# A vision tower on one core: heads of a product-key layer moved between gathering and multiplying, and a scan's sums moved to TensorE

## The reference

```
# 1 tokens: every 4 x 4 patch is averaged; softmax attention of the mean over its 16 pixels, 8 heads
# 2 two-way selective scan, 128 channels, 16 states, over 256 tokens, forward and backward:
for t: h = exp(delta[t] * A) * h + (delta[t] * u[t]) * B[t];  y[t] = sum over 16 states of C[t] * h
# 3 product keys, 8 heads:
scores, idx = top_k(q @ keys of side 0 and of side 1, 16 each of 64)
score = 16 x 16 sums; final_scores, final_indices = top_k(score, 16); softmax
k, v = sum of 16 weights times rows of a table of 4096 rows per head, 64 + 64 wide
out  = causal attention of 256 tokens per head with this k and v, then Wo
```

## Time and profile before

| | |
|---|---|
| median of 3 runs | 13356.86 us (13354.56 to 13362.06) |
| the profiled execution | 13354.71 us, span 13352.6 us |
| TensorE (PE) busy | 11719.0 us, 88% |
| its weight loads (PEld) | 9286.1 us, 70% |
| VectorE (DVE) | 10428.1 us, 78% |
| ScalarE (ACT) | 7363.4 us, 55% |
| GpSimd (POOL) | 10215.8 us, 77%, 9220 instructions |
| mean granted TensorE clock | 0.933 |

### The profile page before, as it was taken

How to read it: one execution, slowest core, us unless ns; L and a number is a source line. 1 busy time by engine, 2 the same in 40 slices (tenths; PEclk the granted TensorE clock), 3 DMA queues, 4 the chain that set the end, 5 groups by cost and what they waited for, 6 DMA issues and landing times.

```text
span 13352.6 us, 262103 instructions
## 1 busy us (share of the span) xinstructions
PE 11719.0 (88%) x71396; PEld 9286.1 (70%) x71396; DVE 10428.1 (78%) x39940; ACT 7363.4 (55%) x17030; POOL 10215.8 (77%) x9220
## 2 busy tenths in 40 slices
PE   3888888988989889989889888898888888898988
PEld 3677677776777767777767677776677677776776
DVE  7878778778778787787777877877878878778772
ACT  2555555555555555555555555555555555555554
POOL 1777777777777777777777777777777777777776
PEclk6999999999999999999999999999999999999999
DMA  2555555555555555555555555555555555555554
GB/s 73 160 145 153 157 145 154 154 144 159 145 151 158 144 154 153 147 156 148 149 159 146 151 159 143 155 154 146 157 143 153 159 145 153 158 142 157 152 140 120
DMA packets 1668219, 1983.98 MB, mean 149 GB/s; under 512 B 532846, under 2 KB 1134062, under 8 KB 1666286
## 3 DMA queue, kind: packets, MB, share of 16 engines
q1 hardware_dynamic: 1371566, 1359.71, 35.8%
q0 software_dynamic: 294912, 604.57, 17.5%
HBM read 1898.00 MB, written 65.01 MB: 147 GB/s over the span
## 4 chain that ended last, share of the span: by engine, by line
PE 38%; DVE 26%; POOL 18%; issue 11%; DMA 4%; ACT 2%; SPq 0%; DVEq 0%; POOLq 0%; ACTq 0%
POOL gath L801 18%; PE bank L991 9%; PE bank L1032 6%; PE bank L873 4%; PE bank L1019 3%; DVE apart L1701 3%; PE bank L1006 3%; DVE row_f L1704 3%; DMA gath<-in_table_dram,rowsT 2%; DVE decay L1576 2%; PE bank L954 2%; DVE onehot L1803 2%; PE bank L977 2%; PE bank L1050 1%; DMA moving<-keyspace 1%
## 5 line engine op out<-in xcount | busy, mean ns | idle before, releaser
L801 POOL DMA_INDIRECT gath<-in_table_dram,rowsT x9216 | 10215.6, 1108 | 3105.9 <-issue 2673.7
L1256 ACT ACTIVATE weight<-bank 128x512 f32<-128x512 f32 x3584 | 2139.3, 597 | 4415.0 <-PE bank L1006 4383.9
L991 PE MATMUL bank<-weight,rowtab 128*128 128x256 f32 x12288 | 3373.8, 399 | 0.0
L1032 PEld LDWEIGHTS bank<-spread,gath 128*128 128x128 f32 x18432 | 2519.7, 201 | 727.8 <-DMA gath<-in_table_dram,rowsT 607.6
L1032 PE MATMUL bank<-spread,gath 128*128 128x96 f32 x18432 | 2524.3, 282 | 519.0 <-DMA gath<-in_table_dram,rowsT 518.8
L991 PEld LDWEIGHTS bank<-weight,rowtab 128*128 128x128 f32 x12288 | 2460.7, 202 | 620.3 <-issue 102.2
L1249 ACT ACTIVATE bank<-bank,seventeen 128x512 f32<-128x512 f32 x3584 | 2370.6, 661 | 13.3 <-PE bank L1006 10.2
L1019 PE MATMUL bank<-moving,pick_b 96*128 96x512 bf16 x3584 | 1457.5, 407 | 304.7 <-ACT bank L1249 226.5
L1006 PE MATMUL bank<-moving,pick_b 96*128 96x512 bf16 x3584 | 1435.0, 400 | 71.1 <-DMA moving<-keyspace 70.6
L1568 DVE TENSOR_TENSOR_SCAN decay<-decay,wide 128x1024 f32<-128x1024 f32 x512 | 1169.3, 2285 | 26.4
L1836 DVE SCALAR_TENSOR_TENSOR acc<-bank,rrow,acc 128x64 f32<-128x64 f32 x1024 | 240.5, 276 | 839.3 <-PE bank L1006 797.2
(11 more groups left out here) (268 smaller groups left out, 18929.9 us busy)
## 6 DMA issues: line engine op xcount, KB each, us to landing
rowtab<-in_tableD_dram SPq DMA_DIRECT2D x2048, 256.0 KB
wide<-states SPq DMA_DIRECT2D x512, 512.0 KB
moving<-keyspace SPq DMA_DIRECT2D x3072, 64.0 KB
gath<-in_table_dram,rowsT POOLq DMA_INDIRECT x9216
pix<-in_x_dram SPq DMA_DIRECT2D x504, 256.0 KB
moving<-keyspace SPq DMA_DIRECT2D x3072, 32.0 KB
keyspace<-split SPq DMA_DIRECT2D x192, 256.0 KB, 2.1
moving<-keyhalf SPq DMA_DIRECT2D x512, 64.0 KB
```

The lines of the kernel that those rows point to most:

```text
L801: pool.indirect_dma_start(out=gath[:, u % RING, j, :], out_offset=None, in_=table, in_offset=bass.IndirectOffsetOnAxis(ap=rowsT[k][:, col: ...
L991: mm(dense_ps[:, 0:TOK], rowtab[:, r, s % 2 * 2 + half, :], weight[s % 2][:, half * TOK:(half + 1) * TOK], start=(s % 16 == 0 and half == ...
L1032: mm(sums_ps[:, col:col + STREAM], gath[:, u % RING, j, :], flat[:, col:col + STREAM], start=True, stop=True)
L1256: ins = af(weight[s % 2][:], zd_ps[s % 2][:], ACT.Exp, scale=-1.0)
```

## The change

`DENSE` goes from 3 to 4: heads 0 to 3 are dense in full (64 slots a period), heads 4 to 7 are gathered (32 parts, 128 fetches). The half head with its own functions, its DRAM buffer `keyhalf`, its semaphores and the items `S.X5`, `S.selh`, `S.l2`, `S.R8`, `S.R9`, `S.wb4`, `k4` and `g4` goes. The number of table tiles streamed stays 32. The gather ring shrinks from 6 parts to 4. In the scan VectorE's half sums (L1577) go, and TensorE sums 32 products (two directions of 16 states), not 16. The four plans are written anew for 64 slots.

```diff
-DENSE = 3
+DENSE = 4
-HU = DU + TILES
+HU = DU
-SLOTS = 16 * DENSE + 8
+SLOTS = 16 * DENSE
-PARTS = (GH * SPAN - SPAN // 2) // PART
-RING = 6
+PARTS = GH * SPAN // PART
+RING = 4
...
                     for r in range(2):
                         hs = decay[r][:, q * 4 * TOK:(q + 1) * 4 * TOK]
-                        after(step(v.tensor_tensor(hs, hs, quarter[q], ALU.mult)))
-                        last = v.tensor_tensor(hs[:, 0:2 * TOK], hs[:, 0:2 * TOK], hs[:, 2 * TOK:4 * TOK], ALU.add)
+                        last = v.tensor_tensor(hs, hs, quarter[q], ALU.mult)
                     last.then_inc(c_done, 1)
...
-                    n = c // 2 * 4 + c % 2
-                    for r in range(2):
-                        mm(scan_ps[:, r * TOK:(r + 1) * TOK], ident[:], decay[r][:, n * TOK:(n + 1) * TOK],
-                           start=(n == 0 and r == 0), stop=False, skip_group_check=True)
+                    for n in (2 * c, 2 * c + 1):
+                        for r in range(2):
+                            mm(scan_ps[:, r * TOK:(r + 1) * TOK], ident[:], decay[r][:, n * TOK:(n + 1) * TOK],
+                               start=(n == 0 and r == 0), stop=False, skip_group_check=True)
...
-                if h < DENSE:
-                    mm(dense_ps[:, 0:TOK], rowtab[:, r, s % 2 * 2 + half, :],
-                       weight[s % 2][:, half * TOK:(half + 1) * TOK],
-                       start=(s % 16 == 0 and half == 0), stop=(s % 16 == 15 and half == 1),
-                       skip_group_check=True)
-                else:
-                    for q in (2 * half, 2 * half + 1):
-                        mm(dense_ps[:, 0:P], rowtab[:, r, q, :], weight[s % 2][:, q * P:(q + 1) * P],
-                           start=(s % 16 == 0 and q == 0), stop=(s == SLOTS - 1 and q == 3),
-                           skip_group_check=True)
+                mm(dense_ps[:, 0:TOK], rowtab[:, r, s % 2 * 2 + half, :],
+                   weight[s % 2][:, half * TOK:(half + 1) * TOK],
+                   start=(s % 16 == 0 and half == 0), stop=(s % 16 == 15 and half == 1),
+                   skip_group_check=True)
```

Of the plans, the lines that the prediction speaks of (TensorE's, VectorE's and SP's):

```diff
 PE_ORDER
-21 z20+0 a0.6+0 o21+0 d19+0 g1.5+0 a1.0+0
-28 z27+0 a1.6+0 o28+0 d26+0 a2.0+0
-39 z38+0 o39+0 d37+0 g3.1+0 S.E1+1
-55 z54+0 o55+0 d53+0 S.E2+1 F.y+2
+0 z63-1 o0+0 d62-1
+16 z15+0 o16+0 d14+0
+25 z24+0 o25+0 d23+0 g1.4+0 a0.6+0
+26 z25+0 o26+0 d24+0 a1.0+0
+33 z32+0 d31+0 o33+0 g2.0+0 a1.6+0 F.t2+2
+34 z33+0 o34+0 d32+0 a2.0+0 S.A0+1 F.xz+2
+41 z40+0 o41+0 d39+0 g2.4+0 a2.6+0 S.E0+1
+61 z60+0 o61+0 d59+0 g3.6+0 F.S6+2
+63 z62+0 o63+0 d61+0 g3.7+0 a5.5+0 S.E2+1 F.y+2
 DVE_ORDER
-51 S.selh+1 F.C3+2
-54 S.lo2+1 a5.5+0 S.R8+1 S.e5+1
+41 S.e1+1
+49 F.sb1+2 a3.5+0
+55 a4.5+0 F.sb3+2
+56 a4.6+0 S.A2+1
+57 F.C2+2 S.wh+1 S.re2+1
+58 S.A3+1 F.C3+2
+61 S.wb0+1 S.e5+1 a5.5+0
 SP_ORDER
-27 m30+0 x7+3
-42 lq0+2 t23+0 m45+0
-44 lq1+2 t24+0 m47+0
-46 lq2+2 t26+0 m49+0
-48 lq3+2 t28+0 m51+0
+50 lq1+2 lq0+2 t27+0 m53+0
+56 lq2+2 t30+0 m59+0
+58 x4+3 x5+3 st1+1 t31+0 lq3+2 m61+0
+63 m2+1
+64 x7+3
```

More of the change, by code:

```diff
@@ L121 @@
[L121 to L125, removed]
-46 z45+0 o46+0 d44+0
[L127 to L134, removed]
-55 z54+0 o55+0 d53+0 S.E2+1 F.y+2
+4 z3+0 o4+0 d2+0 a6.3-1
@@ L136 @@
+52 z51+0 o52+0 d50+0 a4.3+0
+53 z52+0 o53+0 d51+0 g3.2+0
+54 z53+0 o54+0 d52+0
+55 z54+0 o55+0 d53+0 g3.3+0 a4.5+0 F.S0+2
+56 z55+0 o56+0 d54+0 F.S1+2
+57 z56+0 o57+0 d55+0 g3.4+0 a4.6+0 F.S2+2
+58 z57+0 o58+0 d56+0 a5.0+0 F.S3+2 S.A2+1
+59 z58+0 o59+0 d57+0 g3.5+0 F.S4+2 F.S5+2
+60 z59+0 o60+0 d58+0 a5.3+0
+61 z60+0 o61+0 d59+0 g3.6+0 F.S6+2
+62 z61+0 o62+0 d60+0 F.S7+2
+63 z62+0 o63+0 d61+0 g3.7+0 a5.5+0 S.E2+1 F.y+2
 """
 ACT_ORDER = """
-0 w55-1 l0+0 S.E2+0 F.sq2+2
-1 w0+0 K3-1 l1+0 a6.0-1 F.g+1 F.sq3+2
@@ L141 @@
[L141 to L157, removed]
+0 w63-1 l0+0 k3-1 a5.5-1 F.sq2+2 F.sq3+2 S.E2+0
@@ new lines @@
+1 w0+0 l1+0 K3-1
+2 w1+0 S.hi3+0 l2+0 F.g+1 F.sq0+2
+3 w2+0 a6.0-1 l3+0
+4 w3+0 l4+0 F.sq1+2
+5 w4+0 l5+0 S.n+1 S.mi3+0
+6 w5+0 l6+0 a6.4-1 F.kv0+2
+7 w6+0 S.E3+0 l7+0 F.kv1+2 a6.5-1
+8 w7+0 F.kv2+2 l8+0
+9 w8+0 F.kv3+2 S.tb+1 l9+0 S.s0+1
+10 w9+0 F.kv4+2 F.kv5+2 l10+0
+11 w10+0 F.kv6+2 l11+0 F.kv7+2 S.s1+1 a7.0-1
+12 w11+0 l12+0
+13 w12+0 l13+0 F.kv8+2 S.s2+1 F.kv9+2
+14 w13+0 l14+0
+15 w14+0 a7.4-1 F.kv10+2 F.kv11+2 l15+0
+16 w15+0 l16+0 a7.5-1 F.rs0+2 k0+0
+17 w16+0 l17+0 K0+0
+18 w17+0 l18+0 F.t0+2 S.s3+1 a0.0+0
@@ L194 @@
-55 w54+0 k4+0 l55+0 a5.5+0
+27 w26+0 l27+0 a1.0+0
+28 w27+0 l28+0
+29 w28+0 l29+0 F.t1+2
+30 w29+0 l30+0 a1.4+0
+31 w30+0 F.rs1+2 l31+0
+32 w31+0 l32+0 k1+0 a1.5+0 K1+0
+33 w32+0 l33+0 S.wd+1
+34 w33+0 F.t2+2 l34+0 S.ln+1 F.ez+2
+35 w34+0 l35+0 S.hi0+1 a2.0+0
+36 w35+0 l36+0 F.sg+2
+37 w36+0 l37+0
+38 w37+0 l38+0 S.mi0+1 S.hi1+1 a2.4+0
+39 w38+0 l39+0 S.cp+1 F.dt0+2
+40 w39+0 F.xd+2 l40+0 F.dt1+2
+41 w40+0 a2.5+0 l41+0 F.dc0+2
+42 w41+0 S.E0+1 l42+0 S.mi1+1
+43 w42+0 a3.0+0 l43+0
+44 w43+0 l44+0 F.dc1+2
@@ L195 @@
+45 w44+0 l45+0 F.dc2+2
+46 w45+0 l46+0 a3.4+0
+47 w46+0 l47+0 F.dc3+2
+48 w47+0 l48+0 k2+0 F.dc4+2 a3.5+0 K2+0
+49 w48+0 l49+0
+50 w49+0 l50+0 F.dc5+2 S.E1+1
+51 w50+0 l51+0 a4.0+0
+52 w51+0 l52+0 S.wg+1
+53 w52+0 l53+0 F.dc6+2
+54 w53+0 l54+0 F.dc7+2
+55 w54+0 a4.4+0 l55+0
+56 w55+0 a4.5+0 l56+0
+57 w56+0 l57+0
+58 w57+0 l58+0 S.hi2+1
+59 w58+0 l59+0 a5.0+0
+60 w59+0 l60+0
+61 w60+0 l61+0
+62 w61+0 l62+0 a5.4+0
+63 w62+0 l63+0 S.mi2+1
 """
 DVE_ORDER = """
-0 a5.6-1 F.y+1 F.ps+2
-1 S.R9+0 S.e6+0
@@ L249 @@
-51 S.selh+1 F.C3+2
-52 a5.3+0 S.R6+1 S.R7+1
-53 S.re2+1 S.e4+1
-54 S.lo2+1 a5.5+0 S.R8+1 S.e5+1
-55 S.wb1+1
+0 F.y+1 a5.6-1
+1 F.ps+2 F.g+1
+2 S.e6+0 S.e7+0
+3 F.h2+1 S.re3+0
+4
+5 a6.3-1 S.n0+1 S.n1+1 S.lo3+0 S.R7+0
+6 F.rf+2 a6.5-1
+7 a6.6-1 S.T0+1
+8
+9
+10 S.T1+1 S.T2+1 S.T3+1
+11 S.T5+1 S.T4+1
+12
+13 S.T6+1 S.T7+1 a7.3-1
+14 S.T10+1
+15 S.T8+1 S.T9+1 F.var+2 S.wb2+0
+16 S.T11+1 S.T12+1
+17 S.T13+1 a7.5-1
+18 a7.6-1 F.nw0+2 S.T15+1
+19 F.q0+2
+20
+21 a0.3+0 F.q1+2
+22 a0.5+0 S.T16+1
+23 F.q2+2 S.T14+1 F.pv0+2
@@ new lines @@
+24 a0.6+0
+25 S.T17+1
+26 S.cp+1 F.pv1+2 S.T18+1 S.A0+1
+27 F.pv2+2 a1.3+0 S.pr0+1
+28
+29 S.wb3+0 S.L0+1 F.h1+2 S.L1+1
+30 S.L2+1 F.nw1+2 S.L3+1
+31 a1.5+0 S.sel+1 S.wd+1
+32 a1.6+0
+33 S.G0+1 S.wx+1 S.G1+1 S.A1+1
+34 S.G2+1
+35 F.uz0+2 S.G3+1 S.re0+1
+36
+37 S.T19+1 F.uz1+2 S.G4+1
+38 a2.3+0 S.wg+1
+39 S.lo0+1 S.i+1 S.re1+1
+40 S.e0+1 S.pr1+1
+41 S.e1+1
+42 F.dl+2 a2.5+0 S.R0+1 a2.6+0
+43 S.e2+1 S.e3+1 F.B0+2
+44
+45 S.R1+1 F.sf0+2
+46 S.R2+1 a3.3+0
+47 F.sb0+2 F.B1+2 S.lo1+1
+48 F.sf1+2
+49 F.sb1+2 a3.5+0
@@ L254 @@
+50 F.B2+2 a3.6+0 S.e4+1
+51 F.sf2+2 F.C0+2
+52
+53 F.sb2+2 a4.3+0 F.B3+2
+54 F.C1+2 F.sf3+2
+55 a4.5+0 F.sb3+2
+56 a4.6+0 S.A2+1
+57 F.C2+2 S.wh+1 S.re2+1
+58 S.A3+1 F.C3+2
+59 S.R3+1 a5.3+0
+60
+61 S.wb0+1 S.e5+1 a5.5+0
+62 S.R4+1 S.lo2+1 S.R5+1
+63 S.wb1+1 S.R6+1
 """
@@ L267 @@
 10 t7+0 m13+0
-11 m14+0
+11 st2+0 m14+0
 12 t8+0 m15+0
-13 m16+0 x0+3
+13 m16+0
 14 t9+0 m17+0
-15 m18+0 x1+3
-16 t10+0 m19+0
-17 out-1 m20+0 x2+3
+15 m18+0
+16 t10+0 x0+3 m19+0
+17 m20+0
 18 t11+0 m21+0
-19 m22+0 x3+3
+19 m22+0
 20 t12+0 m23+0
-21 m24+0 x4+3
-22 t13+0 m25+0
-23 m26+0 x5+3
+21 m24+0
+22 t13+0 out-1 m25+0
+23 m26+0
 24 t14+0 m27+0
-25 m28+0 x6+3
+25 m28+0
 26 t15+0 m29+0
-27 m30+0 x7+3
+27 m30+0
 28 t16+0 m31+0
@@ L291 @@
 34 t19+0 m37+0
-35 bc+2 m38+0
+35 m38+0
 36 t20+0 m39+0
-37 m40+0
+37 x1+3 m40+0
 38 t21+0 m41+0
 39 m42+0
-40 st0+1 t22+0 m43+0
-41 st1+1 m44+0
-42 lq0+2 t23+0 m45+0
+40 t22+0 bc+2 m43+0
+41 m44+0
+42 t23+0 m45+0
 43 m46+0
-44 lq1+2 t24+0 m47+0
-45 t25+0 m48+0
-46 lq2+2 t26+0 m49+0
-47 t27+0 m50+0
-48 lq3+2 t28+0 m51+0
[L306 to L312, removed]
+44 t24+0 st3+0 m47+0
+45 m48+0
+46 t25+0 m49+0
+47 m50+0
+48 t26+0 x2+3 m51+0
+49 m52+0
+50 lq1+2 lq0+2 t27+0 m53+0
+51 m54+0
+52 t28+0 st0+1 m55+0
+53 m56+0
+54 x3+3 t29+0 m57+0
+55 m58+0
+56 lq2+2 t30+0 m59+0
+57 m60+0
+58 x4+3 x5+3 st1+1 t31+0 lq3+2 m61+0
+59 x6+3 m62+0
+60 t0+1 m63+0
+61 m0+1
+62 t1+1 m1+1
+63 m2+1
+64 x7+3
 """
@@ L1695, in second @@
                         done("pr1")
-                    for other in ("sel", "selh"):
-                        if other in mark:
-                            after(mark[other])
+                    if "sel" in mark:
+                        done("sel")
                     if "R" in mark:
@@ L1725, in second @@
                     mark["i"] = step(v.tensor_copy(idx_b[:], best_i[:, :, 0:HU, :]))
-                if name in ("sel", "selh"):
-                    lo, hi = (0, DU) if name == "sel" else (DU, HU)
-                    for other in ("L" if name == "sel" else "X",):
-                        if other in mark:
-                            after(mark[other])
+                if name == "sel":
+                    lo, hi = 0, DU
+                    if "L" in mark:
+                        done("L")
                     if "R" in mark:
@@ L1788, in second @@
                     side, t = n // 2, n % 2
-                    for other in ("i", "sel", "selh"):
+                    for other in ("i", "sel"):
                         if other in mark:
```

302 lines of the change are left out of this document (94 added, 208 removed).

## The result

The changed kernel takes 13057.44 us (median of 4 runs, 13052.47 to 13067.73) against 13355.71 us in the same job: ratio 0.9777, 95% interval 0.976 to 0.9794. It is 2.2% faster. The forecast was 0.9% and 13,230 us: the direction was right, the time lies in the range, and the size is short by more than half.

What follows compares the result with a forecast made beforehand. The prediction took POOL as the bound, TensorE close behind. Its terms took the period from 203.8 to 202.1 us, -109 over 64 periods, and -15 at the end gave about 13,230 us (0.9% less); eight-in-ten range 12,860 to 13,600.

Steps and rivals of the forecast that it cites:

- gathered rows: TensorE's three waits an image for rows fetched by POOL should go: -8.1 us a period.
- TensorE's work: Eight more slots, half-head products, fewer gathered parts and doubled state sums on TensorE: 3.5 + 6.7 - 3.4 + 7.1 = +13.9 us a period.
- light slots: Slots with z, o and d alone, where z waits for ScalarE's l: nine instead of four, +3.0 us a period.
- attention starts: Each start stands a slot later, so TensorE's wait for the addition into acc shrinks: -3.2 us a period.
- one-hots: TensorE's one-hot wait at S.E2, its last input now planned two slots ahead: -1.8 us a period, bounds -2.6 and +1.
- clock: TensorE's mean granted clock rises from 0.933 with fewer long waits: -5.5 us a period, bounds -7 and 0.
- rival 2: Late load of states: VectorE waits at C0 or C3, or TensorE at o53: +3 a period, 13,420 us, chance 0.13.
- The end: The last image's gathers: 16 fewer fetches save 20 us of POOL, TensorE's longer work takes some back: -15 us.
- The gathers' step: 16 fewer fetches take POOL from 201.4 to 179 us; it stops being the bound, and 8.1 us of waits go.
- the one by which TensorE had room: Weight-load busy time counts, so TensorE's added work vanishes: period 190.2 us, 12,470 us, chance 0.02.
- Rival 1: Clock and waits don't come back while TensorE, the bound, gets more work: +6.8 us a period, 13,770 us, chance 0.21.
- Rival 4: More comes back: clock 7, acc 3.6, one-hots 2.6, light slots nothing: period 196.4 us, 12,865 us, chance 0.14.

Runs made afterwards that it cites:

- vector_sums: The changed kernel with the state sums alone undone (VectorE adds the halves, TensorE sums 16 products): 12644.85 us, 0.9467 of the kernel before.
- keys_spread: The changed kernel with SP's item bc behind keys m44 and B's four quarter loads spread over slots 41, 43, 45, 47: 12790.19 us, 0.9582 of before.
- skip16: The kernel before with four of 36 gathered parts not fetched (128 fetches instead of 144, output not the layer's): 13095.77 us, 0.9802.
- spread_vector: The changed kernel with both B's loads spread as in keys_spread and the state sums back on VectorE: 12543.22 us, 0.9392 of the kernel before.
- starts_same_slot: The changed kernel with six of eight attention starts back in the slot of the previous head's stage .6: 13459.82 us, 1.009 of before.
- tensor_sums: The kernel before with the state sums alone moved (VectorE's half sums gone, TensorE sums 32 products): 13499.27 us, 1.0102.
- keys_first: The changed kernel with keys m43 issued ahead of item bc in SP's slot 40, instead of behind it: 12953.84 us, 0.9693 of before.

## Why the prediction fell short

The terms of its sum, forecast and measured, us per period. A wait is its total before and after, divided by 64.

| term | forecast | measured | from |
|---|---|---|---|
| gathered rows | -8.1 | -8.1 | 518.8 to 0.5 |
| TensorE's work | +13.9 | not measured as a whole; its 7.1 of state sums count 6.4 | vector_sums |
| light slots | +3.0 | +2.8 | wait at z, 226.5 to 403.1 |
| attention starts | -3.2 | -3.5 | 228.0 to 1.4 |
| one-hots | -1.8 | -2.5 | 166.1 to 8.3 (two lines) |
| clock | -5.5 | -8.7 | 0.933 to 0.975, below |
| keys | 0 | +3.1 | 70.6 to 269.9 |
| waits not in the sum | 0 | -1.7 | kvd 68.3 to 0, uz 42.8 to 4.4, wout_g 38.9 to 2.0, prob 3.2 to 38.1 |

With 13.9 for the work they give 199.1, and 199.6 was measured. For the clock: with two levels, 2 x 0.067 of 203.8 us are 27.3 us at 1.2 GHz before, 2 x 0.025 of 199.6 us are 10.0 after, and half of the difference is 8.7. That is an upper estimate, since a low clock costs nothing while TensorE idles. It agrees with the busy times: TensorE's rose by (12064.0 - 11719.0) / 64 = 5.4 us a period, 8.5 less than the 13.9 of new work.

**The step that failed is a size, the clock's.** The prediction bounded it by -7 and took -5.5, on the ground that the waits for gathers were the larger part of the long ones, not all of them. The clock gave back some 8.7. The other long waits went too, and the mean grant after, 0.975, is above the 0.97 of its best stretch, though the longer wait for keys costs clock once an image. Its bound took one stretch of before, which held waits of its own, for the best that is possible.

**Smaller waits were under-counted**, by 0.3 at acc, 0.7 at the one-hots, and by 1.7 that the sum left out. Together with 3.2 at the clock that is 5.9 us; the keys took 3.1 of it back, and of the rest 2.5 show in the period.

**The keys' wait is an error of the other sign.** The prediction went through SP's new order for lq and x and named a late load as rival 2, but of bc it said nothing: it is covered by "every other item keeps its cost". The cost stood in the trace of before (70.6 us of waits for keys), and what made it grow, as far as the timelines show, was ScalarE's copy of xd, planned later against its matmul, and one us less of TensorE's work ahead of the keys. keys_spread prices the burst at 4.2 us a period. The sign that the prediction gave for rival 2, keyspace waits of some hundreds of us, has come, by a load that it did not look at. The loads of C that it did look at were late for VectorE by 56.3 us in all, and TensorE's wait at the S items didn't grow (68.1 to 52.9). Without this miss the forecast would have been farther off: that the time came out as near as it did is in part luck.

**The end** was forecast at -15 and gave -37.5: what goes there is not fetching time alone but TensorE's idling and its low clock too.

**The gathers' step gave the right number for a reason that was half right.** That POOL alone held the old plan is refuted by skip16: relieved of as many fetches it gains 2.0%, and VectorE holds TensorE at the S items instead. The 8.1 us come back in the changed kernel together with a plan in which VectorE is punctual. The sentence that the half sums buy punctuality "at the end of the period" falls too: with them on VectorE the new plan is as punctual, and 413 us faster.

**Right were** POOL with idle time that ends on TensorE, gath under 1 us a period, acc under 60 us in total, L1001 at 16384 instructions, the price of the light slots, that a smaller ring is hidden at this period, and TensorE as the bound: work taken from it counts at 0.9. The limit of that cover was set too low: the prediction put it at a period under 179 us, and at 191.5 us (spread_vector) TensorE waits for rows again. Not met were TensorE's busy share, 92% of the span where 94 to 96% were expected, and L920's busy time (now L931), 975.8 us and not twice 604.1. Of the rivals, the one by which TensorE had room, with a chance of 0.02, is refuted by the same run. Rival 1's price came from doubting the clock; the clock came back. Rival 4 was nearest in its mechanism: it asked for 13.2 us from clock, acc and one-hots together, and they gave 14.7. Its period of 196.4 us was missed because the light slots and the keys took 2.8 and 3.1.

Left open: how the gain divides between spacing, order and the even spread of parts g. starts_same_slot gives 6.3 us a period for the starts, of which 2.4 (155.9 / 64) belong to the edit, while 4.2 of keys' wait went away in it, so the price is not a clean one. And why tensor_sums costs 2.3 us of 7.1 was read from waits and the clock, not tested. The differences from the changed kernel are taken across jobs, in which the median of the kernel before lay between 13349 and 13356 us.

## What to carry to other kernels

Where two engines are late at the same point, removing one's wait shows the other's: before a wait is booked as a gain, ask who is next at that instruction. Move work to the engine with room, and look again after each half of a change; here the half that moved sums to TensorE took back 413 of the 709 us that the rest of the change gives without it. In a queue that waits and issues in order, a small urgent load should not stand behind a burst of big ones: spreading four loads over eight slots was worth 2.0%. Such a burst can lie almost hidden in the old plan, so when a plan is written anew, compare for each load how long before its use its source is ready.

## What the runs showed of the hardware

The mean granted clock rose as TensorE's idle time fell (span less busy time, us a period): 0.933 at 25.5 (before), 0.937 at 23.6 (skip16), 0.943 at 22.9 and 0.947 at 20.0 in the old plan with the sums moved, 0.965 at 18.4 (starts_same_slot), 0.975 at 15.4 (after), 0.985 at 12.5 (keys_spread). vector_sums (0.973 at 15.5) fits in; keys_first (0.976 at 13.5) and spread_vector (0.979 at 14.2) stand in the other order. That is a relation over ten kernels, each profiled once, not a cause tested by itself. In single places: the keys' wait of 1.73 us before left the clock at 1.00 (6142 to 6154 us), the one of 4.71 us after had 0.70 in it and 0.73 behind it, and in skip16 a wait of 6.91 us at the first S item had 0.67 behind it (6088 to 6098 us).

On the DMA side, for the 5 us of the keys' wait all engines were taken (share 1.01, 287 GB/s), against 0.56 in the mean of the period, and the matmul that needed these 96 KB of keys started 8.5 us after the issue of their second part. Before, the same burst showed a share of 1.05 at 325 GB/s.
